# Second attention of a four-stage kernel: partial output products of two tiles placed ahead of the value products of the last two rounds

## The reference

```python
x = x + attention0(cond0(x, style))
x = x + ffn0(cond1(x, style))
x = x + attention1(cond2(x, style))      # the step of this case
x = x + ffn1(cond3(x, style))
```

```python
q = rmsnorm(x @ wq_a.T) @ wq_b.T                     # per head 64 plain and 64 rotary columns
ckv, k_pe = split(x @ wkv_a.T)                       # 32 latent and 64 rotary columns
k_nope, v = split(rmsnorm(ckv) @ wkv_b.T)
attn = softmax(causal(q_full @ k_full.T * scale))
return (attn @ v).reshape(B, S, 32 * 128) @ wo.T
```

## Time and profile before

| | us |
|---|---|
| median of three runs | 1003.07 |
| lowest and highest | 1001.19, 1003.25 |
| the profiled execution, its own time | 1000.5 |
| its span, from first to last instruction | 998.7 |

### The profile page before, as it was taken

The page is one execution under the profiler, slowest core; times in us unless marked ns, Lnnn a source line. Parts: engine busy times, 40 slices in busy tenths (PEclk is TensorE's granted clock), DMA queues, the critical chain, the costliest instruction groups (busy, mean ns, idle before and its releaser), DMA issues.

```text
span 998.7 us, 15964 instructions
## 1 busy us (share of the span) xinstructions
PE 953.3 (95%) x6766; PEld 708.3 (71%) x6766; DVE 556.3 (56%) x951; ACT 232.4 (23%) x451; POOL 469.3 (47%) x425
## 2 busy tenths in 40 slices
PE   5899998999999999999999999989989999899997
PEld 2337886877887778877888788737857777446853
DVE  7866747557285672947629644434148978203323
ACT  4602112211122111222121200110161666400001
POOL 7934538486574855758557613201223545220300
PEclk9999999999999999999999999989999999899999
DMA  5782101211102111011111392693460000082002
GB/s 139 175 255 68 58 1 43 74 43 54 44 1 74 43 53 43 29 46 43 53 43 43 86 210 96 129 208 111 147 232 1 3 3 3 1 174 59 4 1 84
DMA packets 36287, 74.30 MB, mean 74 GB/s; under 512 B 13492, under 2 KB 22260, under 8 KB 33140
## 3 DMA queue, kind: packets, MB, share of 16 engines
q1 hardware_dynamic: 35880, 72.89, 26.1%
q10 hardware_dynamic: 336, 0.39, 0.1%
HBM read 66.26 MB, written 7.01 MB: 73 GB/s over the span
## 4 chain that ended last, share of the span: by engine, by line
PE 70%; DVE 10%; POOL 9%; ACT 4%; DMA 3%; issue 3%; SPq 1%; POOLq 0%; DVEq 0%
PE ps L1164 14%; PE ps L1232 11%; PE ps L1025 8%; PE ps L1488 6%; PE ps L1306 6%; PE ps L1178 4%; POOL w_lo L2390 3%; DVE arena L2043 3%; DMA acts<-level_rows 2%; ACT acts L1533 2%; PE ps L1311 2%; PE ps L1411 2%; DVE arena L2040 1%; PE ps L1413 1%; PE ps L1412 1%
## 5 line engine op out<-in xcount | busy, mean ns | idle before, releaser
L2505 POOL TENSOR_TENSOR arena<-arena 128x512 f32<-128x512 f32 x80 | 103.5, 1294 | 123.3 <-DVE arena L2043 123.2
L1164 PE MATMUL ps<-xt_hi,w_hi 128*128 128x512 f32 x320 | 127.7, 399 | 5.8 <-POOL w_lo L2390 2.7
L1164 PE MATMUL ps<-xt_lo,w_hi 128*128 128x512 f32 x320 | 125.5, 392 | 0.0
L1164 PE MATMUL ps<-xt_hi,w_lo 128*128 128x512 f32 x320 | 125.4, 392 | 0.0
L2043 DVE TENSOR_TENSOR arena<-ps,rope 64x512 f32<-64x512 f32 x160 | 110.2, 689 | 2.2
L2061 DVE TENSOR_TENSOR fresh<-ps,fresh 128x512 f32<-128x512 f32 x56 | 38.7, 691 | 119.7 <-PE ps L1232 119.6
L1232 PE MATMUL ps<-h_hi,wo_lo 128*128 128x512 f32 x224 | 82.1, 395 | 1.4 <-POOL wo_lo L2512 1.4
L1232 PE MATMUL ps<-h_hi,wo_hi 128*128 128x512 f32 x224 | 82.8, 400 | 0.0
L1232 PE MATMUL ps<-h_lo,wo_hi 128*128 128x512 f32 x224 | 81.9, 396 | 0.0
L1164 PEld LDWEIGHTS ps<-xt_hi,w_hi 128*128 128x128 f32 x320 | 60.0, 188 | 24.2 <-DVE arena L2043 4.7
L2413 POOL TENSOR_TENSOR xt<-arena 128x512 f32<-128x512 f32 x16 | 20.3, 1269 | 119.4 <-DVE arena L1948 119.4
(11 more groups left out here) (338 smaller groups left out, 1947.5 us busy)
## 6 DMA issues: line engine op xcount, KB each, us to landing
acts<-in_w_o_dram SPq DMA_DIRECT2D x8, 1024.0 KB, 5.1
arena<-in_a_wo_dram SPq DMA_DIRECT2D x8, 1024.0 KB, 6.3
arena<-kernel_rows SPq DMA_DIRECT2D x11, 512.0 KB, 11.8
acts<-in_w_qkv_dram SPq DMA_DIRECT2D x3, 1792.0 KB, 7.1
acts<-in_w_qkv_dram SPq DMA_DIRECT2D x4, 1280.0 KB, 6.7
w_l<-kernel_rows SPq DMA_DIRECT2D x10, 512.0 KB, 12.0
arena<-level_rows SPq DMA_DIRECT2D x3, 1024.0 KB, 21.1
stream<-in_x_dram SPq DMA_DIRECT2D x4, 512.0 KB, 6.5
```

What stands on the lines that cost most here:

```text
L1164: last = pe.matmul(ps[:, bank, :], w[:, r, cols], x, start=(r == 0 and n == 0), stop=(r == R - 1 and n == 2))
L2505: pool.tensor_tensor(qk[:, chunk, half * HALF:(half + 1) * HALF], rot[:, k % 2, 0, :], rot[:, k % 2, 1, :], ALU.add).then_inc(s_rope, 1)
```

## The change

The only code that changes is PE's list in `attention1`. The function `out_tile` is defined earlier. In the loop passes i = 6 and i = 7, just ahead of `pv(5)` and `pv(6)`, PE now makes the output products of groups 0 to 4 for tile 0 (bank 6) and tile 1 (bank 7). Ahead of the first of them stand three waits: all 64 query tiles rotated (banks 6 and 7 are free of them), all 16 latent query tiles copied, and ten head halves copied (groups 0 to 4 present). After the loop, tiles 0 and 1 get groups 5 and 6 only. Number and kind of the matmuls stay as they were; ten of them move.

```diff
@@ -1466,6 +1466,13 @@
+                def out_tile(n, groups):
+                    half, r_out = n // 4, n % 4
+                    for i in groups:
+                        last = pe.matmul(ps[:, OUT1[n], :], wcomb[:, i, r_out, :],
+                                         latent(i)[:, half * HALF:(half + 1) * HALF], start=(i == 0), stop=(i == 7))
+                    return last
+
@@ -1475,6 +1482,12 @@
                     if i + 2 < 8:
                         queries(i + 2, range(5))
+                    if i == 6:
+                        pe.wait_ge(s1_rot, 64)
+                        pe.wait_ge(s1_lat, 16)
+                        pe.wait_ge(s1_head, 10)
+                    if i >= 6:
+                        out_tile(i - 6, range(5))
                     if i:
                         pv(i - 1)
@@ -1482,19 +1495,12 @@
                 for n in range(6):
                     if n == 3:
                         pv(7)
-                    out_tile(n, range(7))
+                    out_tile(n, range(0 if n >= 2 else 5, 7))
```

More of the change, by code:

```diff
@@ L1483, in attention1 @@
                         scores(i + 1)
[L1485 to L1490, removed]
                 pe.wait_ge(s_pull, SOFT0 + 16)
```

## The result

| | before | after |
|---|---|---|
| median of seven runs, us | 1001.19 | 992.44 |
| lowest and highest, us | 996.0, 1003.25 | 990.46, 999.54 |
| profiled execution, its own time, us | 1000.5 | 992.14 |
| its span, us | 998.7 | 990.4 |
| mean granted clock of PE | 0.990 | 0.995 |

The ratio of the times is 0.9915, with a 95% interval of 0.9893 to 0.9936: between 6.4 and 10.7 us less. Measured once more later, the change gave 0.9912 (0.9887 to 0.9937). The 999.54 us is one run, in which PE's mean granted clock was 0.987; in the other six it was 0.995 to 0.998.

What follows compares the result with a forecast made beforehand. PE, busy 95% of the span, was taken as the bound; 4.89 us of waits, 2.79 of clock and 0.2 of restarts make 7.9, taking the median from 1003.07 to 995.2 us, range 992.4 to 998.2.

Steps and rivals of the forecast that it cites:

- The steps on PE: PE from 840.33 us: tile 0 starts without a wait, pv(5) at 844.72, pv(6) at 855.07, pv(7) at 867.35.
- a sum of 7.9: Total gain up to pv(7): 4.89 us of waits, 2.79 of clock and 0.2 for four pipeline restarts.
- The waits: PE's four idle pieces ahead of pv(5) and pv(6), waiting for ACT's probabilities, would go: 4.89 us.
- the 0.81: PE's wait for ACT's head copy after pv(6), ahead of the output products, would stay at 0.8 us.
- The clock's 2.79: Full PE clock in pv(6)'s second half (0.86 us) and the first eight output records (1.93) would give back 2.79 us.
- The late scores: scores(7) on PE starts 2.15 us late, shifting round 7's softmax; cost taken as zero, with 4.0 us of cover left.
- the bound of 1.2 us: Upper bound if ACT runs both exponentials of round 7 (1.18 us) in front of pv(6)'s head copies.
- The load path: The next stage's transfers, issued after pv(7), shift together with their need at L1025; 10 us of slack stay.
- 998.0: Rival: the clock in this stage stays as dear as before, so only 5.1 us are gained; chance 0.11.
- The waits did not move to `pv(7)`: Rival: round 7's softmax comes much later, pv(7) waits again and the gain is gone, 1003 us; chance 0.04.
- The slower rival: pv(7) holds up tile 3 and the next stage's transfers, slower from 877.3 us on; chance 0.02.
- The forecast of 995.2: Median total time in us: 1003.07 before, less the stage's gain passed through to the end; chance 0.83.

Runs made afterwards that it cites:

- filled kernel: The kernel before, with useless matmuls in PE's waits ahead of the halves of pv(5) and pv(6), no output product moved; time ratio 0.997 (0.9952 to 0.9988).
- tile 0 alone: Against the kernel before, only tile 0's five products moved, ahead of pv(5); 73.13 us from round 6's last score block to the first L1025.
- four tiles early: Against the kernel before, groups 0 to 4 of tiles 0, 1, 4 and 5 moved ahead of pv(5); 74.24 us from round 6's last score block to L1025.
- tile 1 alone: Against the kernel before, only tile 1's five products moved, ahead of pv(6); 72.60 us from round 6's last score block to the first L1025.
- ACT's copies first: Only tile 0 moved, plus pv(6)'s head copies ahead of round 7's exponentials on ACT; 69.62 us from round 6's last score block to L1025.

## Why the prediction was right

- **The steps on PE** held. `pv(5)` was forecast 5.41 us after the start of the last score block and came 5.51 after it. For `pv(6)` it was 15.76 and 15.83, for `pv(7)` 28.04 and 28.20. The start of tile 0 needed no wait. The stage gained 7.76 us against a sum of 7.9.
- **The parts of the sum.** The waits went, 4.89 us, and the 0.81 stayed, as forecast. The clock's 2.79 was right for the profile it was read from, and the filled kernel shows that it hangs on the waits. My reading of where the clock fell was off: windows of 2 us have it at 1.00 up to 852 us and at 0.54 behind, so it fell with the fourth wait, not after the third. And the 2.79 was wrong as a constant of the kernel: place and length of the fall differ between executions, and it cost 0.9 to 3.4 us in three. The stage before took 75.22 to 77.73 us, so the change is worth 6.4 to 8.9 us, depending on which execution it is compared with. The sum meets the measured 7.76 within 0.2 us because both are taken against the same profile.
- **The late scores.** The sum held that no head copy is held back. In the changed kernel that is so. The exponentials ended at 854.6 and the first copy waited for PE until 855.89. They came 1.4 us later than before against the last score block, not 2.1 as forecast, since before they had stood behind `spread(6)`, which ran until they began:

```profile
853.43 1.18 ACT L1744 ACTIVATE arena<-arena 128x512 f32<-128x512 f32 x2 [1.46 <-POOL arena L2473]
855.89 0.60 ACT L1764 ACTIVATE w_l<-ps 128x512 f32<-128x512 f32 x1 [1.28 <-PE ps L1460]
```

  But the bound of 1.2 us that I gave this cost was too low for what the mechanism can do. Where the products of tile 1 don't stand between, the same order on ACT costs 1.8 us of wait and 1.7 of clock (tile 0 alone). I had counted the exponentials' length only, not ACT's idle time in front of them, nor the clock behind.
- **The load path** shifted with `pv(7)`, as forecast, and had more slack than it needed: even with 8.6 us less between `pv(7)` and L1025 nothing waited.
- **The rivals.** The clock was given back, so 998.0 did not come, and the filled kernel speaks against a fall that has nothing to do with the waits. The waits did not move to `pv(7)`, in any run; what moves, when products are placed otherwise, is the wait for the head copies. The slower rival lost its ground in the run with four tiles early.
- **The level.** The forecast of 995.2 used the median of three runs of before, 1003.07. Over seven it is 1001.19, 1.9 lower, and the gain was 8.75 us instead of 7.9. Together that puts the measured 992.44 2.8 us below the forecast and only 0.04 above the low end of the range, 992.4. The mechanism was right; that the time lies inside the range is luck. The 8.75 are 1.0 more than the stage gave in the profiles. Runs of one kernel scatter by several us, so that this 1.0 is real is not shown; a longer fall in the runs of before would be one cause, and the falls outside the stage are another.

## What to carry to other kernels

When an in-order engine waits in several short pieces for a chain on other engines, put work there whose inputs are ready, and then follow the chain that the work delays through every engine's list: the cost shows where a copy stands behind the delayed step, not where the delay began. Price the clock together with the waits, since short waits in a row can bring it down and the dense work behind them pays. And compare stages between two fixed instructions: that length repeated here to 0.01 us in the changed kernel, where the clock stayed up, while whole runs scattered by 6 to 9.

## What the runs showed of the hardware

Short waits in a row went with a fall of the clock to its lower level. It fell with gaps of 0.79 and 1.28 us (tile 1 alone), and did not fall after a single wait of 1.24 us in a filled stream, of 0.81 in the changed kernel, or of 0.76 and 0.81 in the run with ACT's copies first. Where it falls, and for how long, differs between executions of the same program, in this stage and at 40, 600 and 660 us. Much of the scatter of the timed runs goes with the clock: of 13 runs of the kernel before on one chip, the four with a mean clock of 0.987 took 1003.46 to 1004.62 us, and the two with 0.992 took 998.60 and 999.19. The difference of 0.005 of some 1000 us is 5 us, and the times differ by about that. Filling the waits of one stage does not end this: the changed kernel's seven runs lie between 990.46 us at a mean clock of 0.998 and 999.54 us at 0.987.
